# Tridiagonal reduction inside a fused graph network: p formed and transposed in two halves

## What is computed

```python
h = jnp.maximum(_layernorm(x, axis=-1), 0.0)
x = x + _L0_gnn_ref(h, adj, ...)      # L_norm from adj; _, U = jnp.linalg.eigh(L_norm); U (relu(U^T h W1 + b1) W2 + b2)
h = jnp.maximum(_layernorm(x, axis=-1), 0.0)
x = x + _L1_gnn_ref(h, adj, ...)      # two graph convolutions, then four short LSTMs over windows
```

## Time and profile before

| | us |
|---|---|
| median of the three runs shown | 1660.71 |
| the profiled execution's own time | 1660.92 |
| its span, first to last instruction | 1658.9 |
| DVE busy in the span | 1259.3 (76%) |
| PE busy (matmul) | 1289.4 (78%) |
| ACT, POOL busy | 609.9, 397.7 |
| two-block steps 1 to 126 | from 24 to 477 |
| granted TensorE clock up to 477 us | full |

### The profile page before, as it was taken

One profiled execution on the slowest core, in us unless ns is written; L12 is line 12 of the kernel. 1 busy time (PEld: TensorE's weight loads), 2 busy tenths in 40 slices (PEclk: granted clock), 3 DMA queues, 4 the chain that ended last, 5 costly groups with the idle time before them and its releaser, 6 DMA issues.

```text
span 1658.9 us, 25312 instructions
## 1 busy us (share of the span) xinstructions
PE 1289.4 (78%) x5985; PEld 1068.8 (64%) x5985; DVE 1259.3 (76%) x6154; ACT 609.9 (37%) x2116; POOL 397.7 (24%) x2138
## 2 busy tenths in 40 slices
PE   6999999999976667777264444519878899999997
PEld 5777888888865555555143333507656588889897
DVE  7898988888888888888999999993732255555555
ACT  1222222222233444222121212402223386868676
POOL 5333333333345555555100000120000011000100
PEclk9999999999999999999887775769989999999999
DMA  7000000000000000000000000000000000000001
GB/s 166 1 1 1 1 1 1 2 1 1 2 1 1 1 1 1 1 1 1 0 1 0 1 0 1 1 0 1 1 1 1 0 1 1 1 1 26 1 27 52
DMA packets 23402, 12.64 MB, mean 8 GB/s; under 512 B 5075, under 2 KB 22230, under 8 KB 23254
## 3 DMA queue, kind: packets, MB, share of 16 engines
q1 hardware_dynamic: 23254, 11.03, 2.7%
HBM read 6.83 MB, written 4.19 MB: 7 GB/s over the span
## 4 chain that ended last, share of the span: by engine, by line
DVE 47%; PE 33%; issue 9%; POOL 6%; ACT 4%; DVEq 1%; POOLq 0%
PE bank L873 10%; PE bank L875 6%; DVE A L1001 4%; DVE RC L1089 4%; PE bank L647 3%; DVE O L1097 3%; PE bank L650 3%; DVE O L983 3%; DVE pa L1085 3%; DVE O L1093 2%; DVE junk L953 2%; DVE zc L995 2%; DVE wk L987 2%; PE bank L791 2%; PE bank L818 2%
## 5 line engine op out<-in xcount | busy, mean ns | idle before, releaser
L592 ACT ACTIVATE H<-bank,gate_b 128x128 f32<-128x128 f32 (+2 forms) x624 | 213.4, 438 | 81.9 <-PE bank L875 79.3
L650 PEld LDWEIGHTS bank<-O 128*128 128x128 f32 x764 | 201.3, 344 | 0.0
L873 PE MATMUL bank<-O,WlT 128*128 128x128 f32 (+1 forms) x896 | 192.0, 328 | 7.8 <-DVE O L1366 5.6
L659 PE MATMUL bank<-O,y 128*128 128x2 f32 x510 | 142.4, 349 | 65.5 <-DVE y L953 59.7
L647 PE MATMUL bank<-ident,O 128*128 128x128 f32 x382 | 148.2, 457 | 47.6 <-DVE O L983 35.6
L467 ACT ACTIVATE ncp<-pc,RC 128x2 f32<-128x2 f32 (+1 forms) x254 | 74.9, 295 | 292.4 <-DVE RC L974 292.4
L659 PEld LDWEIGHTS bank<-O,y 128*128 128x128 f32 x510 | 128.4, 312 | 77.5 <-issue 72.4
L875 PE MATMUL bank<-H,WlT 128*128 128x128 f32 (+2 forms) x768 | 169.1, 301 | 0.0
L873 PEld LDWEIGHTS bank<-O,WlT 128*128 128x128 f32 x896 | 148.1, 192 | 24.6 <-issue 7.3
L650 PE MATMUL bank<-O 128*128 128x1 f32 x764 | 162.7, 305 | 0.0
L667 PE MATMUL bank<-ident,pc 128*128 128x128 f32 x381 | 147.7, 456 | 5.4 <-DVE pc L972 2.2
(11 more groups left out here) (381 smaller groups left out, 3059.2 us busy)
## 6 DMA issues: line engine op xcount, KB each, us to landing
X<-in_x SPq DMA_DIRECT2D x2, 2048.0 KB, 13.9
out<-X SPq DMA_DIRECT2D x32, 128.0 KB, 1.9
adj_sb<-in_adj SPq DMA_DIRECT2D x1, 256.0 KB, 3.0
W1s<-in_L_gnn_W SPq DMA_DIRECT2D x1, 64.0 KB, 10.2
W2s<-in_L_gnn_W SPq DMA_DIRECT2D x1, 64.0 KB, 3.2
Wg0s<-in_L_gnn_Wg SPq DMA_DIRECT2D x1, 64.0 KB, 3.0
Wg1s<-in_L_gnn_Wg SPq DMA_DIRECT2D x1, 64.0 KB, 3.6
Wl<-in_L_gnn_Wih SPq DMA_DIRECT2D x1, 0.5 KB, 6.6
```

The costliest lines, as they stand in the source:

```text
L592: ins = a(gates[:, q, i, 0:n], gate_at(p, q, i), fn, bias=gate_b[:, p - 1, i:i + 1])
L650: ins = mm(bank[0][:, 0:1], R[:, b, k, 0:1].to_broadcast([P, P]), R[:, b, k, 0:1], start=(b == bl[0]), stop=(b == 1))
L659: ins = mm(sb_[:, 0:2], y[:, 1:2].to_broadcast([P, P]), R[:, 1, k, :], start=True, stop=(k >= P - 1))
L873: last = mm(gate_at(p, q, i), WlT[:, 0, p - 1, i, :], window(c, p, t, part), start=True, stop=(t == 0))
```

## The change

In a two-block step the pivot scalar `pb` is formed between the two dot products instead of behind the upper y. The lower half of p, `pc[:, 1:2]`, is then formed on its own behind the second dot and ahead of the upper y, with a semaphore of its own (`p1_ready`), and PE transposes it between the two y.x products. The upper half of p stays at its old place, one column wide, and PE transposes it last. One-block steps keep their order.

```diff
                 if k < P - 1:
+                    pe.wait_ge(S["p1_ready"], k + 1)
+                    nc.tensor.transpose(bank[5][:, P:N], pc[:, 1:2].to_broadcast([P, P]), idf)
                     pe.wait_ge(S["y0_ready"], k + 1)
                     ins = mm(sb_[:, 0:2], y[:, 0:1].to_broadcast([P, P]), R[:, 0, k, :], start=False, stop=True)
                 ins.then_inc(S["s_ready"], 1)
                 if not last:
                     pe.wait_ge(S["p_ready"], k + 1)
-                    for b in bl:
-                        ins = nc.tensor.transpose(bank[5][:, b * P:(b + 1) * P], pc[:, b:b + 1].to_broadcast([P, P]), idf)
-                    ins.then_inc(S["prow_ready"], 1)
+                    b = bl[0]
+                    nc.tensor.transpose(bank[5][:, b * P:(b + 1) * P], pc[:, b:b + 1].to_broadcast([P, P]), idf).then_inc(S["prow_ready"], 1)
...
+                def pivot():
+                    dve.wait_ge(S["half_ready"], k + 1)
+                    dve.wait_ge(S["root_ready"], k + 1)
+                    tt(pb, root[:], half[:], ALU.mult).then_inc(S["pb_ready"], 1)
+
                 for b in reversed(bl):
                     e = P if b == 0 else N
+                    if b == 0:
+                        pivot()
                     if k:
                         dve.wait_ge(S["upd1" if b else "upd0"], k)
                     v.tensor_tensor_reduce(out=junk2[:, b, c0:e], in0=A[:, b, c0:e], in1=xb[:, c0:e], scale=1.0, scalar=0.0,
...
                 if b0 == 0:
+                    dve.wait_ge(S["y1_ready"], k + 1)
+                    dve.wait_ge(S["pb_ready"], k + 1)
+                    stt(out=pc[:, 1:2], in0=A[:, 1, c0:c0 + 1], scalar=pb, in1=y[:, 1:2], op0=ALU.mult, op1=ALU.subtract, reverse1=True).then_inc(S["p1_ready"], 1)
                     dve.wait_ge(S["y_part"], k + 1)
                     dve.wait_ge(S["y01_ready"], k + 1)
                     stt(out=y[:, 0:1], in0=bank[6][:, 0:1], scalar=below[:, 0, k:k + 1], in1=y[:, 0:1], op0=ALU.mult, op1=ALU.add).then_inc(S["y0_ready"], 1)
-                dve.wait_ge(S["half_ready"], k + 1)
-                dve.wait_ge(S["root_ready"], k + 1)
-                tt(pb, root[:], half[:], ALU.mult).then_inc(S["pb_ready"], 1)
+                else:
+                    pivot()
...
-                    stt(out=pc[:, bs], in0=A[:, bs, c0], scalar=pb, in1=y[:, bs], op0=ALU.mult, op1=ALU.subtract, reverse1=True).then_inc(S["p_ready"], 1)
+                    stt(out=pc[:, b0:b0 + 1], in0=A[:, b0, c0:c0 + 1], scalar=pb, in1=y[:, b0:b0 + 1], op0=ALU.mult, op1=ALU.subtract, reverse1=True).then_inc(S["p_ready"], 1)
```

More of the change, by code:

```diff
@@ L178, in gnn_kernel @@
             lt_rdy adjT_rdy adjT_cp wlt_ps wlt_cp biases
-            x_ready xrow_ready sig_ready root_ready g1_ready y_part y01_ready y0_ready y1_ready half_ready pb_ready p_ready c_ready
+            x_ready xrow_ready sig_ready root_ready g1_ready y_part y01_ready y0_ready y1_ready half_ready pb_ready p_ready p1_ready c_ready
             xm_ready ym_ready vt_ready v_ready kc_ready ncp_ready sy_ready yb_ready t_ready s_ready prow_ready cx_ready gq_ready w_ready z_ready add0 add1 upd0 upd1 s_hist d0_ready seed_rdy half_upd
```

## The result

The changed kernel takes **1669.12 us** (median of 4 runs, 1666.96 to 1669.9) against 1660.78 us of the kernel before, measured beside it: a ratio of 1.0051, 95% interval 1.0033 to 1.0068. It is 8.3 us slower. The forecast was 1669, 8 us slower.

A forecast was written before the change was run, and what follows sets the result against it. DVE was taken to bound early two-block steps and PE late ones; with the root's wait setting the upper y from about step 35, gains of 2.2 and 0.1 against losses of 4.2 and 6.2 gave 8 us slower, 1669 us, range 1661 to 1677.

The forecast's parts named there:

- The ring: Two-block steps, x to x: DVE sets early steps, PE late ones; root ends 1.81 after x, x 1.29 after upper y.
- Transposing the lower half earlier, wk 0.16 earlier: Start of two-block steps: the wait for transposed p goes, wk starts 0.15 after x; a gain where DVE sets the step.
- Pivot scalar, 0.10 behind the root: Between the dots on DVE: pb starts 0.10 after the root's end, with second dot, lower p and upper y queued behind.
- Upper y = pb + 0.39: DVE, every two-block step: lower p starts 0.25 behind pb, the upper y 0.14 behind that.
- Behind the upper y and PE, zero: From upper y to x: still 1.29; PE's early transposition booked at zero, bounds 0 to 0.16 a step.
- The sum: Steps 1 to 31 gain 2.2 us, 32 to 47 about 0.1; 48 to 87 lose 4.2, 88 to 126 lose 6.2.
- the clash: On PE, a rival: early transposition holds the upper y's product, 20 us on top, 1689, or half, 1679; chance 0.10.
- Rival 2: Lower p costs only its place in DVE's list: upper y 0.39 to 0.44 after the root, about 1663; chance 0.13.
- Rival 4: DVE waits for its place at the second dot, not the root: 0.07 gained every step, 1652; chance 0.11.

The follow-up runs named there:

- the last run: Changed order with the fastest kernel's choice of carried waits, the lower p carrying its wait for pb, against the kernel before: 1647.1 us, ratio 0.9923.
- The fastest kernel: Kernel before, waits exchanged so instructions carry the one ending last, except one-block steps' tm and x, which keep theirs: 1635.47 us, ratio 0.9849.

## Why the prediction was right, point by point

- *The ring*: right. The root ends 1.82 to 1.86 behind x in every kernel without the added delay; POOL's chain puts x 1.28 behind the upper y (1.22 to 1.31, by stretch, where the carried waits were exchanged).
- *Transposing the lower half earlier, wk 0.16 earlier*: the size is right in late steps (0.15 behind x), where it is worth nothing, and 0.03 short in early ones. The cause is only partly right: 0.09 of it comes from the pivot scalar, since p no longer waits for `pb` (`wk` 0.21 behind x in the two runs that transpose both halves last), and 0.03 to 0.06 from the early transposition. This is also the term that was mis-sized: 31 x 0.07 = 2.2 us forecast, 1.2 measured. In an early step after the change

```profile
105.28 0.19 POOL L317 TENSOR_TENSOR kc<-NG,RC 128x1 f32<-128x1 f32 x1
...
105.37 0.26 DVE L993 SCALAR_TENSOR_TENSOR O<-cx,gqn,tm 128x2 f32<-128x2 f32 x1
105.42 0.19 POOL L322 TENSOR_TENSOR vt<-ident,NG 128x2 f32<-128x2 f32 x1
...
105.55 0.21 DVE L997 SCALAR_TENSOR_TENSOR wk<-bank,gqn,kc 128x1 f32<-128x1 f32 x1
```

  `wk` stands 0.18 behind x and not 0.15, because x itself lasts 0.26 and not 0.22. I had taken the gap from kc's end and not asked how long x holds DVE. In steps 4, 7 and 8, where x lasts 0.22, `wk` does stand 0.14 behind it, and the step is 0.08 to 0.09 shorter than before; where x lasts 0.25 or more it is mostly 0.04 to 0.05.
- *Pivot scalar, 0.10 behind the root*: right, 0.10 to 0.11 in the late steps of every kernel with the pivot ahead of the upper y (in the changed one from step 33 on), and 0.03 in the last run, where the instruction carries that wait; shown to be the bound by the delayed root.
- *Upper y = pb + 0.39*: 0.40, and shown by the exchanged wait to be on the ring.
- *Behind the upper y and PE, zero*: right. The run with both transpositions last excludes the clash.
- *The sum*: +8 forecast, +8.3 measured. Late and middle stretches were right to 0.2 us; the gain of steps 1 to 31 was 1.0 us too high and that of steps 32 to 47 0.4 too low, errors that partly cancel. Part of the agreement is luck: straight lines through steps 49, 77 and 120 give means of 0.09 and 0.145, 3.7 and 5.7 us, where the sum used 0.105 and 0.16 and so came to 8 instead of 7. The measured means are 0.10 and 0.16. The rare stalls of about 0.3 us hardly count: there are 13 in either trace.

Rival 2 (the lower p costs only its place) fails: the upper y stands 0.50 behind the root's end (453.73, 454.23), not 0.39 to 0.44. It had a real part in that the pair shrinks when the wait is carried, to 0.22, and to 0.20 in late steps of the last run, but not to the 0.13 to 0.14 of independent instructions. By the section "The DRAIN you can't avoid" of the Trainium skill's page "VectorE: DVE Perf Modes" a semaphore after each of eight chained copies costs nothing. For operations of one element a partition these runs do not agree: g, which waits for `pb`, starts 0.25 to 0.26 behind it in the kernel before and 0.19 with the wait carried, and independent ones start 0.13 to 0.14 apart. Rival 4 (the root is not waited for) is right only up to about step 32, as its own condition said.

## What to carry to other kernels

Idle time ahead of an instruction is no free room for one that waits for something else: ask when that other thing is there. Here 0.33 us of idle time stood behind a dot, but the root ended only after that dot's start, so the pivot scalar moved that idle time ahead of itself and put the second dot, the lower p and the upper y behind it. An early stretch and a late one of the same loop can have different bounds, so price a change at several steps and sum. And where an instruction waits for two semaphores, let it carry the one that ends last, and read again which that is after each exchange: two of the exchanges here sat on waits that had become the last, and cost 8 us until they were taken back.

## What the runs showed of the hardware

- A wait that is a separate small instruction, when it ends last, costs 0.07 us on DVE: root to `pb` 0.10 before and 0.03 with the wait carried, `pb` to g 0.26 and 0.19 (medians of the one-block steps). At the lower p of the changed kernel it was 0.04 (0.26 and 0.23). On POOL it costs 0.06, not the 0.1 that I had expected: upper y to ym 0.36 before (453.42, 453.78) and 0.30 with it carried:

```profile
436.02 0.22 DVE L961 SCALAR_TENSOR_TENSOR y<-bank,below,y 128x1 f32<-128x1 f32 x1 [0.38 <-PE bank L655]
...
436.32 0.20 POOL L309 TENSOR_TENSOR ym<-y,below 128x2 f32<-128x2 f32 x1 [1.75 <-DVE y L961]
```

- In two-block steps of the two kernels without exchanged waits x (DVE) and POOL's vt mostly start 0.05 to 0.06 apart, and one of them is longer: x 0.22 with vt 0.22 (the late step of the changed kernel, 451.91), or x 0.26 with vt 0.19 (its early step, 105.37). When x is the longer one, the root is at 1.85 to 1.86 instead of 1.82. The fastest kernel has other distances between the two. Of its 127 two-block steps, x lasts 0.22 in all 44 in which vt starts earlier than x or less than 0.02 behind it, 0.24 to 0.25 in the 10 with 0.04, and 0.26 in most of those with 0.05 to 0.06: a longer x ends 0.20 behind vt's start, that is with vt. One of them:

```profile
437.01 0.26 DVE L983 SCALAR_TENSOR_TENSOR O<-cx,gqn,tm 128x2 f32<-128x2 f32 x1
437.07 0.19 POOL L322 TENSOR_TENSOR vt<-ident,NG 128x2 f32<-128x2 f32 x1
```

  So a POOL operation that starts 0.03 to 0.06 behind a small DVE one can make it up to 0.04 longer. The page "SBUF — State Buffer" of the Trainium skill, section "SBUF: two separate sides", has Vector and GpSimd share a pair of ports as an exclusive lock, for a DVE operation with two SBUF inputs against a GpSimd one that reads SBUF. The lengths fit a wait of that kind, but no run here took POOL's vt away or moved its operands, so the lock stays an explanation.
